# Gated cross-mixing and a mixture of experts on one core: weights and contexts stored turned in memory, and the first expert's eight pieces loaded and split between tiles 20 and 30 of the first stage

## The reference

```python
def _L0_xattn_ref(x, adj, W, b):          # x: the context, adj: the normalised rows
    si = jnp.einsum('bnd,d->bn', x, Wi[0])
    sj = jnp.einsum('bnd,d->bn', x, Wj[0])
    xij = jax.nn.sigmoid(si[:, :, None] + sj[:, None, :] + b[0])
    return P_ASEM * xij + (1.0 - P_ASEM) * adj
...
def _L0_ffn_ref(x, wg, W, b):
    logits = xt @ wg
    idx = jnp.argmax(jax.nn.softmax(logits, axis=-1), axis=-1)
    expert_out = jnp.einsum('nh,eoh->neo', xt, W) + b[None, :, :]
    out = jnp.einsum('ne,neo->no', onehot * gate, expert_out)
...
x = x + jnp.tanh(g_xattn[0]) * _L0_xattn_ref(ctx_512, _layernorm(x, axis=-1), L0_xattn_W, L0_xattn_b)
x = x + jnp.tanh(g_ffn[0]) * _L0_ffn_ref(_layernorm(x, axis=-1), L0_ffn_wg, L0_ffn_W, L0_ffn_b)
```

## Time and profile before

| what | us |
|---|---|
| three runs: lowest, median, highest | 680.94, 691.27, 696.54 |
| profiled execution, span from the first to the last instruction | 687.3 |
| median less that span | 4.0 |
| first stage: last router matmul ends at | 184.2 |
| first matmul of the loop at | 211.2 |
| last matmul of the loop ends at | 669.0 |
| PE, DVE, ACT, POOL busy | 576.6, 445.2, 274.1, 331.8 |

### The profile page before, as it was taken

How to read it: one execution, slowest core, us unless ns; L and a number is a source line. 1 busy time by engine, 2 the same in 40 slices (tenths; PEclk the granted TensorE clock), 3 DMA queues, 4 the chain that set the end, 5 groups by cost and what they waited for, 6 DMA issues and landing times.

```text
span 687.3 us, 14019 instructions
## 1 busy us (share of the span) xinstructions
PE 576.6 (84%) x2841; PEld 461.2 (67%) x2842; DVE 445.2 (65%) x557; ACT 274.1 (40%) x408; POOL 331.8 (48%) x489
## 2 busy tenths in 40 slices
PE   7898889888707969979779997995999799699990
PEld 5576667666505848858567885884888588588870
DVE  3357778697699885856784587588378557843420
ACT  2367766686424333413333333333343233333220
POOL 1446777788623336325336533633633364356540
PEclk8569999999957989989989998997999899899995
DMA  7911577576679876764776497577756656545530
GB/s 262 403 40 33 175 261 237 198 217 223 239 258 259 238 214 190 225 208 152 224 220 196 147 243 213 189 219 215 217 168 204 189 166 198 164 132 186 182 126 13
DMA packets 83666, 134.72 MB, mean 196 GB/s; under 512 B 11568, under 2 KB 64304, under 8 KB 83504
## 3 DMA queue, kind: packets, MB, share of 16 engines
q1 hardware_dynamic: 73712, 99.47, 49.4%
q0 software_dynamic: 9792, 33.82, 12.8%
HBM read 99.44 MB, written 35.91 MB: 197 GB/s over the span
## 4 chain that ended last, share of the span: by engine, by line
PE 27%; DVE 23%; issue 19%; ACT 9%; POOL 7%; DMA 6%; DVEq 3%; POOLq 2%; ACTq 2%; SPq 1%
PE pair L1058 12%; DVE wt L782 7%; PE pair L985 4%; DVE xr L718 4%; ACT wt L598 4%; DVE pair L777 4%; PE pair L996 3%; PE pair L969 3%; PE pair L974 3%; ACT rb L617 2%; DVE rows L804 2%; DMA out_x<-rows,scatter_row 2%; DMA rows<-table 1%; DVE xc_tr L725 1%; POOL out_x L500 1%
## 5 line engine op out<-in xcount | busy, mean ns | idle before, releaser
L1058 PE MATMUL pair<-wt,xt 128*128 x1728 | 416.2, 404 | 62.6 <-DVE rows L804 41.6
L1058 PEld LDWEIGHTS pair<-wt,xt 128*128 128x128 f32 x1728 | 336.9, 196 | 141.5 <-issue 66.5
L488 POOL TENSOR_TENSOR rows<-rows,rb 128x1024 f32<-128x1024 f32 x37 | 88.7, 2398 | 164.2 <-ACT rb L617 162.6
L782 DVE TENSOR_TENSOR wt<-pair,wt 128x1024 f32 (+1 forms) x64 | 77.5, 1212 | 32.7 <-ACT wt L598 32.7
L598 ACT ACTIVATE wt<-pair 128x1024 f32 (+1 forms) x64 | 64.2, 1024 | 77.7 <-DVE pair L777 70.1
L604 ACT ACTIVATE xt<-pair 128x1024 fp32r<-128x1024 f32 x38 | 39.0, 1026 | 133.0 <-DVE pair L790 110.6
L777 DVE STREAM_TRANSPOSE pair<-w_raw 128x1024 f32<-128x1024 f32 x64 | 79.7, 1250 | 1.9
L790 DVE STREAM_TRANSPOSE pair<-xb 128x1024 f32<-128x1024 f32 x38 | 47.7, 1255 | 46.5 <-issue 26.3
L804 DVE SCALAR_TENSOR_TENSOR rows<-pair,scal,rows 128x1024 f32<-128x1024 f32 x36 | 46.0, 1278 | 44.6 <-PE pair L1058 44.2
L617 ACT ACTIVATE rb<-bias_bc,scal 128x1024 f32 (+1 forms) x37 | 46.0, 1244 | 48.4 <-POOL scal L485 41.1
L794 DVE TENSOR_TENSOR xt<-pair,xt 128x1024 fp32r<-128x1024 f32 x38 | 46.4, 1221 | 28.1 <-ACT xt L604 25.9
(11 more groups left out here) (123 smaller groups left out, 417.9 us busy)
## 6 DMA issues: line engine op xcount, KB each, us to landing
w_raw<-in_L_ffn_W SPq DMA_DIRECT2D x256, 128.0 KB
xb<-table SPq DMA_DIRECT2D x156, 128.0 KB
rows<-table SPq DMA_DIRECT2D x38, 520.0 KB
xr<-in_x SPq DMA_DIRECT2D x32, 512.0 KB, 6.9
ctx_in<-in_ctx SPq DMA_DIRECT2D x8, 512.0 KB, 4.9
bias_bc<-in_L_ffn_b SPq DMA_DIRECT2D x8, 512.0 KB
out_x<-rows,scatter_row POOLq DMA_INDIRECT x36, 4.2
table<-xr,pos POOLq DMA_INDIRECT x32, 4.5
```

What stands on the lines that cost most here:

```text
L488: nc.gpsimd.tensor_tensor(rows[:, k, 0:H], rows[:, k, 0:H], rb[:, :], ALU.add).then_inc(base_ready, 1)
L782: nc.vector.tensor_tensor(where[:, :, 1].rearrange("p a k o -> p (a k) o"), ps[:, :].rearrange("p (k o) -> p k o", k=K), where[:, :, 0].re ...
L1058: last = nc.tensor.matmul(out_ps[r % 2][:, HALF * h:HALF * (h + 1)], xt[:, r % RING, x_part, k, :], wt[:, bass.ds(par, 1), w_part, k, HALF ...
```

## The change

The arrays of weights and contexts are handed to the kernel in another order of elements (the values are the same, and this permutation is not in the measured time): W as expert, inner index in the order of the 32x32 blocks, output; the context as group, column, block of columns, row. A piece of weights is now 128 inner rows by all 1,024 outputs and is loaded with one DMA of 512 KB instead of four of 128 KB. PE's context turning, ACT's context copies and DVE's weight turning are gone. ACT and DVE cut the pieces straight from `w_raw` in SBUF. The contexts have a ring of three instead of two. Since a piece is now a block k, `multiply` goes over k outside and h inside. The first expert's pieces 0 to 3 are loaded by SP in front of x tiles 20 to 23, pieces 4 to 7 behind the x tiles, and piece m is cut at the end of tile 22+m by ACT and DVE.

```diff
 def load_piece(e, m):
-    for q in (0, 2, 1, 3):
-        sp.dma_start(w_raw[32 * q:32 * (q + 1), m % WR, :, :],
-                     in_blocks(W[bass.ds(e, 1), P * m:P * (m + 1), :].rearrange("a o h -> (a o) h"),
-                               q)).then_inc(w_landed[m % WR], 16)
+    sp.dma_start(w_raw[:, m % WR, :], W[bass.ds(e, 1), P * m:P * (m + 1), :]
+                 .rearrange("a h o -> (a h) o")).then_inc(w_landed[m % WR], 16)
...
 for t in range(RX, T):
     sp.wait_ge(row_stored[slot_of(t)], 16)
+    if RX + 4 <= t < RX + 4 + WR:
+        load_piece(0, t - RX - 4)
     sp.dma_start(xr[:, slot_of(t), 0:H], tile_of(x_t, t)).then_inc(x_landed[slot_of(t)], 16)
-for m in range(WR):
-    load_piece(0, m)
 for m in range(WR, K):
-    sp.wait_ge(w_turned, m - WR + 1)
+    sp.wait_ge(w_ready, m - WR + 1)
     load_piece(0, m)
...
 # ACT, at the end of tile t
-    if r == 0 and g + 3 < NG:
-        context_copy(g + 3)
     if r == 2 and g + 3 < NG:
         context_sums(g + 3)
+    if T - K - 2 <= t < T - 2:
+        cut_high(0, t - (T - K - 2), 0)
...
 # DVE, at the end of tile t
+    if T - K - 2 <= t < T - 2:
+        cut_low(0, t - (T - K - 2), 0)
...
+def cut_low(e, m, par):
+    dve.wait_ge(w_hi_ready, K * e + m + 1)
+    where = wt[:, bass.ds(par, 1), :, m, :].rearrange("p a n o -> p (a n) o")
+    nc.vector.tensor_tensor(where[:, 1, :], w_raw[:, m % WR, :], where[:, 0, :].bitcast(F32),
+                            ALU.subtract).then_inc(w_ready, 1)
...
 def sum_context(g):
-    pe.wait_ge(ctx_copied, g + 1)
+    pe.wait_ge(ctx_landed[g % CR], 16 * (g // CR + 1))
+    if g:
+        pe.wait_ge(sj_ready, g)
+        pe.wait_ge(si_ready, g)
...
 def multiply(t, r, e, par):
-    for h in range(2):
-        pe.wait_ge(w_ready, K * e + K // 2 * (h + 1))
-        for k in range(K):
+    for k in range(K):
+        if k % (K // 2) == 0:
+            pe.wait_ge(w_ready, K * e + k + K // 2)
+        for h in range(2):
```

More of the change, by code:

```diff
@@ L28, in build @@
     K = H // P
-    DC = D // P
     TB = S // P
@@ L571, in logits_copy, with cut_high @@
                 nc.scalar.activation(lgt, lgt_ps, ACT.Copy).then_inc(lgt_copied, 1)
-            for g in range(2):
-                context_copy(g)
+            def cut_high(e, m, par):
+                act.wait_ge(w_landed[m % WR], 32 * e + 16 * (m // WR) + 16)
+                nc.scalar.activation(wt[:, bass.ds(par, 1), 0, m, :].rearrange("p a o -> p (a o)"),
+                                     w_raw[:, m % WR, :], ACT.Copy).then_inc(w_hi_ready, 1)
             for g in range(2):
@@ L618, in scaled_bias @@
                                      ACT.Identity, bias=scal[:, k, 3:4], scale=scal[:, k, 6:7]).then_inc(rb_ready, 1)
-            for m in range(4):
-                cut_high(0, m, 0, (cut_a, pair[1])[m % 2])
-            cut_high(0, 4, 0, cut_a)
-            cut_high(0, 5, 0, pair[1])
             xt_high(0, 0, cut_b)
-            cut_high(0, 6, 0, cut_a)
-            cut_high(0, 7, 0, pair[1])
             exp_sum(0, 0)
@@ L902, in pieces @@
                     def pieces(e, first, par, behind_first):
+                        behind_first()
                         for m in range(first, first + K // 2):
-                            turn_weights(e, m, (cut_b, cut_a)[m % 2], m - first)
-                            if m == first:
-                                behind_first()
-                            else:
-                                cut_low(e, m - 1, par, (cut_b, cut_a)[(m - 1) % 2])
-                        cut_low(e, first + K // 2 - 1, par, cut_a)
+                            cut_low(e, m, par)
                         settled(w_ready, K * e + first + K // 2)
@@ L951, in _ @@
             pe.wait_ge(masks_ready, 1)
[L953 to L964 removed]
             def sum_context(g):
[L967 removed]
+                pe.wait_ge(ctx_landed[g % CR], 16 * (g // CR + 1))
+                if g:
+                    pe.wait_ge(sj_ready, g)
+                    pe.wait_ge(si_ready, g)
                 for d in range(DC):
[L969 removed]
+                    last = nc.tensor.matmul(sj_sum(g), wj_bc[:, d, :], ctx_tr[:, g % CR, d, :, :],
                                             start=(d == 0), stop=(d == DC - 1))
@@ L973, in sum_context @@
                     for d in range(DC):
-                        last = nc.tensor.matmul(si_sum(g)[:, c:c + 1], ctx_turned_home(g)[:, c, d, :], wcol[:, d:d + 1],
+                        last = nc.tensor.matmul(si_sum(g)[:, c:c + 1], ctx_tr[:, g % CR, d, c, :], wcol[:, d:d + 1],
                                                 start=(d == 0), stop=(d == DC - 1))
@@ L1086 @@
         a = np.ascontiguousarray(inputs[name])
+        if name == "ctx_512":
+            b, s, d = a.shape
+            a = np.ascontiguousarray(a.reshape(b, 128, 2, 4, d // 128, 128).transpose(0, 2, 5, 4, 3, 1)
+                                     .reshape(2 * b, 128, d // 128, 512))
+        if name == "L0_ffn_W":
+            e, o, h = a.shape
+            a = np.ascontiguousarray(a.reshape(e, o, 4, h // 128, 32).transpose(0, 3, 2, 4, 1).reshape(e, h, o))
         arrays[f"in_{name}"] = a
```

112 lines of the change are left out of this document (23 added, 89 removed).

## The result

The changed kernel takes 631.96 us (median of 4 runs, 630.23 to 632.38), the kernel before in the same runs 688.67 (4 runs, 680.94 to 696.54). The ratio is 0.922, with a 95% interval from 0.9155 to 0.9286: faster, and 10 us slower than the 622 forecast. The profiled execution took 632.38 us for a span of 630.3, so 2.1 us lie around the span and not 4.0.

What follows compares the result with a forecast made beforehand. PE was taken to bound the kernel, busy 84% of 687.3 us, with loop waits for DVE's `finish`. From 687.3 the terms gave 619.8, or 623.8 with 4.0 around the span; the pace check said 619. Forecast 622, range 604 to 648.

Steps and rivals of the forecast that it cites:

- signs for "right": Loop in one or two stretches, 400 us, clock 1.00, waits under 8; tile 0 at 29-31; tiles 22-30 in 38-42.
- (1): Loop: 10.0 us less DVE work per slot pair removes all PE waits for `finish`, -41.6 us; weak end -28.
- (2): Loop: eight slow clock starts of 1.7 us each go with the waits, -13.6 us, between -8 and -18.
- (3): Loop: fewer DMAs for the same weights cost 0, up to +4 us; the new matmul order costs 0.
- C: Loop: the matmuls' new order makes PE change PSUM banks more often; at 170 ns per change 708 us; chance 0.02.
- (4): Opening: tile 0 at 29.4 instead of 36.85, -7 us; -4 if x's landing holds it, -12 if the clock rises.
- (5): Tiles 4 to 19: context turning gone, 2.5 us in each of four groups, -10 us, weak end -4.
- (6): Tiles 22 to 29: first expert's cuts make 5.0 us per tile, +9 us (+2 to +14); early weight loads +1.
- (7): Between the stages: first expert's turning and cutting gone, last store lands sooner, -5.3 us; -2 if the store isn't faster.
- Rival A: Loop: DVE's SBUF cuts and POOL's work exclude each other; half in series 648 us, chance 0.12; all 679, 0.02.
- Rival B: Tiles 22 to 29 at 6.5 us each, +21 instead of +9, and x tiles wait, +4: 637 us; chance 0.12.
- D: Loop: ACT's cuts start late behind POOL's scalars, DVE isn't overloaded; 4 of 10 us saved; 645 to 650; chance 0.04.

Runs made afterwards that it cites:

- experiment 9: Experiment 8's kernel with DVE's `finish` moved ahead of the one-column maximum in every loop slot: 615.54 us, ratio 0.8915.
- experiment 1: Changed kernel with the matmuls' order put back, output halves outside and blocks k inside, waiting for all eight pieces at once: 633.83 us, ratio 0.9222.
- experiment 4: Kernel before with only the contexts' half of the change, weights as before: 673.77 us, ratio 0.9819.
- Experiment 3: Changed kernel with all first-expert cuts moved behind the last tile, loads of pieces 0 to 3 left in place: 625.9 us, ratio 0.9119.
- Experiment 8: Changed kernel with first-expert cuts in DVE's gaps: DVE's in tiles 26 to 31 and behind, ACT's in tiles 24 to 31: 623.07 us, ratio 0.9044.
- experiment 6: Changed kernel with a useless block transpose on DVE put ahead of each of its cuts in the loop: 693.85 us, one run.

## Why the prediction was right, and where its terms were not

The direction and the range held; the forecast was 10 us too low. The sum said 619.8 for a span that came out at 630.3. What was missing is 9.4 us of waits, 5.0 of a slower pace and 3.5 in the ring; 3.7 more in the opening, 1.1 in tiles 4 to 20 and some 2.3 in stages that no term was for went the other way. Of the signs for "right", only the first matmul of the loop (197.4 for "near 199") came as written: the loop went in five stretches and 416 us, with 9.4 us of waits, tile 0 at 26.2 and tiles 22 to 30 in 44.5. None of the signs for "wrong" came (cuts 1.22 us, pace 11.20, the router's last matmul at 175.4). By its own terms:

(1) *Waits.* -32.2 instead of -41.6. The step "10.0 us less is enough for each of them, by 2.9 us for the worst" was mis-sized in three ways. First, DVE's path got shorter by 4.1 to 7.5 us a pair, and not by 10.0. From the turning of the rows to `finish`, the second slot of a pair went from 17.0 us (404.32 to 421.32) to 12.95 (368.83 to 381.78), and gained 3.7 to 4.3 in every pair. The first slot of a pair gained only 0.2 to 3.6 in the six pairs behind the first (at slot 4 it went from 16.6 to 15.9): DVE waits there for ACT's cuts, which stand behind POOL's scalars, 5.4 us now and 3.5 before, when two turnings lay ahead of the wait (both at slot 4). Second, there are eight waits but seven pairs: the pair of slots 8 and 9 had two, 4.48 and 4.04, so the worst lateness was 8.5 and not 7.1; that pair gained 4.1 and kept waits of 2.24 and 1.22. Third, the stand of 2 to 6 us once in six slots, which was already in the trace of before (1.9 to 6.0 us, five times) and which I had not looked for: ahead of the longest wait it was 1.90 us before and 4.41 after. The weak end of -28 came near for a reason that holds in part. Each wait left does stand behind a maximum that took 1.1 to 1.9 us, and experiment 9 takes 3.2 to 5.6 us of the waits away by moving the finish past it. But such holds were nothing that the change adds: all eight waits of before stood behind one of 1.9 to 2.4 us, and in all slots together they cost 22.3 us before and 20.7 after.

(2) *Clock.* -13.6 was said for eight slow starts at 1.7 us, and -13.7 was measured; that the two agree is luck. The 1.7 us of the earlier trace rows were among the cheapest of the eight and not what came "after each wait". The window behind the wait of 7.12 us in the kernel before, with the columns of the earlier trace rows:

```profile
476.42:488.00 11.58, 11.58 (x40) 0.77 0.68 214
```

That one cost (1 - 0.77) x 11.58 = 2.7 us, and the eight together, worked out in the same way, 17.1. Two are left, behind the waits of 2.24 and 5.09 us, with 3.4 us together. For the latter the granted clock was 0.67 over 5.2 us, so (1 - 0.67) x 5.2 = 1.7 us:

```profile
432.80:438.00 5.20, 5.20 (x16) 4.14 (x17) 3.22 (x4) 1.52 (x4) 3.22 (x8) 0.67 0.84 286
```

Behind the waits of 0.81 and 1.22 us it stayed at 1.00. Waits (-32.2), slow starts (-13.7), half a microsecond less at the loop's first matmuls and a slower pace in 24 of the 36 slots (+5.0) sum to -41.4, which is what was measured.

(3) *Transfers and order.* 0, as said; C fell with experiment 1.

(4) *Opening.* -10.7 instead of -7, inside -4 to -12, by the reason given for the low end: the clock rose early, within the second of the three sums. The first two sums' 512-column matmuls took 3.75 us, the third's 1.96, and the one-column matmuls (L907) went from 3.41 in the first to 2.17 in the second and 1.84 in the third.

```profile
15.77 3.75 PE L902 MATMUL pair<-ctx_tr,wj_bc 128*128 128x512 f32 x4 [0.35 <-ACT si_half L520]
21.84 1.96 PE L902 MATMUL pair<-ctx_tr,wj_bc 128*128 128x512 f32 x4 [0.35 <-ACT si_half L520]
```

In the runs with turned contexts tile 0 began between 23.8 and 29.6. In the two at the ends of that range the second sum's matmuls took 1.95 us (23.8), and all three sums' took 3.75 (29.6).

(5) *Context turning.* -11.1, said -10; experiment 4 shows the same 70.64 us with the contexts alone.

(6) *The ring.* A turn was said to be 5.0 us, by the chain `add_tanh`, square, copy, two cuts, and is 5.07. The term was mis-sized all the same, +13.5 instead of +9 and +1: "8 x 5.0 = 40 against 31" took all tiles for plain ones. Four of the eight have `choose` or `position` on DVE as well, which no longer fit beside anything; these four take 3.9 us more than plain ones, 1.2 of it by the slow clock in tile 25, which I had priced in the loop and not here. Experiment 3 shows that the cuts, ACT's and DVE's together, are the whole cause. Experiment 8 shows that most of it is DVE's: with ACT's halves in six of these tiles and DVE's in four, in its gaps, 33.6 us are left of the 44.5. A run with ACT's eight halves alone was not made.

(7) *Between the stages.* -5.0, said -5.3.

Around the span 2.1 us lay where 4.0 were carried over.

Rival A in its half form (648) did not come: the cuts' mean is 1221 ns. Its mechanism is there, though, at the price of other instructions than the cuts. The Trainium skill, page "SBUF — State Buffer", section "Who interferes with whom", says that a DVE instruction with two SBUF inputs and a GpSimd instruction that reads SBUF exclude each other for whole instructions. The rows agree on both sides (POOL's addition of 3.00 us beside a cut, against 2.39 without; the maximum that ends with the addition), and with turnings between the cuts it costs the cuts themselves 14 x 0.9 us. Rival B named the right place with too high a price (its ring +21); the result lies between the forecast and its 637. D said that ACT's cuts start late, behind POOL's scalars, so that 4 of the 10 us are saved per pair. That is what the first slots of the pairs show, and 4.1 to 7.5 saved per pair is nearer to its figure than to mine. Its time (645 to 650) did not come, since a pair's lateness had been 5.9 us on average (41.6 / 7), so that less than 10 was enough for most. Its denial that DVE has too much to do fell with experiment 6. No run moved ACT's cuts ahead.

What stays open: between tile 30 and the loop, version 3 gave back 6.8 us, and which of DVE's eight cuts there carried it was not tried. Nor was it shown what makes an engine stand when the loop turns back, or what sets the pace.

## What to carry to other kernels

Work taken off an engine that others wait for is worth its waits and the slow starts behind them; work moved elsewhere must be weighed against that engine's own row at the new place, tile by tile: a cut of 1.2 us cost 1.7 us per tile where VectorE was full, and about 0.5 in gaps four tiles later (for eight cuts 2.6 us in tiles 22 to 30 and 1.1 behind them). Work taken off an engine is worth its full time only where that engine doesn't wait for another in the same stretch: 5.0 us off each slot gave 0.2 to 4.3. Ahead of an instruction that the bounding engine waits for, put nothing that can be held up by another engine, however small: 0.15 us of work carried 1 to 2 us of waiting. Look at all rows of a kind before one is taken as the price: the slow start used here was among the cheapest of eight. An experiment that puts the suspected cost back tells cause from coincidence, and its surplus (here 16 us more waits than before) must be taken apart before it is named: the contention in plain sight had in fact shrunk, and the order of the work had grown the path.
